# Moving normalizations to ScalarE and sums to GpSimd in a software-pipelined chain of five attentions

## What is computed

```
x1 = LN(x + attention(x, x, causal))            16 heads of 16, rows that are all zero masked
x2 = LN(x1 + attention(x1, ctx))                16 heads of 16
x3 = LN(x2 + (relu(x2 W1 + b1) W2 + b2) * mask)
F, C = LN(x3), LN(ctx)                          the second layer, one head of 256
cross = gelu(softmax(F C') C w1 + c1) w2 + c2
N = LN(cross);  x4 = F + gamma2 * (cross + gamma1 * softmax(N N') N)
x5 = x4 + softmax(x4 ctx') ctx                  the third layer
x6 = x5 + (attention(LN(x5), LN(ctx)) Wo + bo)  8 heads of 32, with biases on q, k, v
u = (LN(x6) Win + bin) B;  s_t = silu(s_{t-1} A') + u_t;  out_t = x6_t + s_t C + mod
```

## Time and profile before

| | before |
|---|---|
| median of 3 runs | 4716.2 us (4705.2 to 4717.8) |
| the profiled execution | 4694.8 us, its span 4693.0 us |
| mean granted TensorE clock | 0.964 |
| busy: PE, DVE, ACT, POOL | 93%, 81%, 59%, 46% |
| before the first group's work / the scan | to about 95 us / from about 4440 us |

### The profile page before, as it was taken

How to read it: one execution, slowest core, us unless ns; L and a number is a source line. 1 busy time by engine, 2 the same in 40 slices (tenths; PEclk the granted TensorE clock), 3 DMA queues, 4 the chain that set the end, 5 groups by cost and what they waited for, 6 DMA issues and landing times. The chain is left out here.

```text
span 4693.0 us, 129503 instructions
## 1 busy us (share of the span) xinstructions
PE 4387.4 (93%) x38563; PEld 3708.0 (79%) x38563; DVE 3780.6 (81%) x10021; ACT 2753.0 (59%) x5761; POOL 2151.9 (46%) x2308
## 2 busy tenths in 40 slices
PE   2899999999999999999999999999999999999758
PEld 1678888888888888888888888888888888887647
DVE  2688888888888888888888888888888888888523
ACT  0466665666666666665666666666666666566411
POOL 0245444444444444444444554444444444454325
PEclk9899999999999999999999999999999999999879
DMA  3000000000000000000000000000000000000045
GB/s 93 17 22 27 29 17 28 26 29 22 24 26 29 29 17 26 29 19 26 26 29 17 29 26 29 17 28 26 29 28 18 29 26 27 18 26 23 16 133 199
DMA packets 139568, 156.21 MB, mean 33 GB/s; under 512 B 23941, under 2 KB 126666, under 8 KB 134858
## 3 DMA queue, kind: packets, MB, share of 16 engines
q1 hardware_dynamic: 139210, 152.93, 10.7%
HBM read 115.01 MB, written 37.88 MB: 33 GB/s over the span
## 5 line engine op out<-in xcount | busy, mean ns | idle before, releaser
L875 ACT ACTIVATE prob<-prob 128x512 f32<-128x512 f32 x1280 | 782.1, 635 | 663.7 <-DVE prob L1030 662.6
L1019 DVE TENSOR_REDUCE mx<-bank 128x4 f32<-128x512 f32 x1280 | 844.5, 682 | 82.0 <-PE bank L598 73.4
L1283 POOL TENSOR_TENSOR rs_ln<-ve_ln,half 128x2 f32<-128x2 f32 x320 | 225.8, 706 | 1436.2 <-DVE ve_ln L998 1436.1
L1030 DVE TENSOR_TENSOR prob<-bank,mx 128x512 f32<-128x512 f32 x1280 | 851.7, 683 | 26.0 <-PE bank L628 7.6
L865 ACT ACTIVATE turned<-bank 128x512 f32<-128x512 f32 x960 | 546.6, 597 | 521.5 <-PE bank L550 400.5
L885 ACT ACTIVATE probT<-bank 128x512 f32<-128x512 f32 x1280 | 722.8, 601 | 179.7 <-PE bank L628 165.0
L628 PE MATMUL bank<-ident,prob 128*128 128x128 f32 x5120 | 780.4, 293 | 13.0 <-ACT prob L875 9.2
L628 PEld LDWEIGHTS bank<-ident,prob 128*128 128x128 f32 x5120 | 627.9, 151 | 104.9 <-issue 46.2
L1330 POOL TENSOR_SCALAR scan_u<-turned,half_of 128x512 f32<-128x512 f32 x256 | 399.4, 1570 | 134.7 <-ACT turned L865 134.7
L1292 POOL TENSOR_TENSOR X<-X,row_ln_g 128x512 f32<-128x512 f32 x192 | 245.5, 1279 | 316.1 <-DVE X L1007 316.1
L598 PE MATMUL bank<-scan_u,turned 32*128 32x256 f32 x4096 | 380.2, 406 | 5.4 <-POOL scan_u L1330 4.9
(11 more groups left out here) (210 smaller groups left out, 8664.7 us busy)
## 6 DMA issues: line engine op xcount, KB each, us to landing
X<-in_x SPq DMA_DIRECT2D x64, 256.0 KB, 3.6
XR<-in_x SPq DMA_DIRECT2D x64, 256.0 KB, 3.8
CB<-in_ctx SPq DMA_DIRECT2D x64, 256.0 KB, 3.6
CC<-in_ctx SPq DMA_DIRECT2D x64, 256.0 KB, 2.6
mod<-mod_rows SPq DMA_DIRECT2D x64, 256.0 KB, 3.4
residual<-X SPq DMA_DIRECT2D x64, 256.0 KB, 3.5
turned<-residual SPq DMA_DIRECT2D x16, 1024.0 KB, 6.8
out<-turned SPq DMA_DIRECT2D x16, 1024.0 KB, 4.8
```

The costliest lines, as they stand in the source:

```text
L875: nc.scalar.activation(flat(t), flat(t), ACT.Exp, scale=SCALE[p]).then_inc(*st["act"].mark(f"exp.{b}{r}"))
L1019: nc.vector.tensor_reduce(m[:], banks.of(f"{att}.tile.{b}{r}")[:, :].rearrange("p (h t) -> p h t", h=4), AX, ALU.max)\
L1030: nc.vector.tensor_tensor(t[:], banks.of(f"{att}.tile.{b}{r}")[:, :].rearrange("p (h t) -> p h t", h=4), maxes.of(f"{att}.max.{b}{r}")[:]. ...
```

## The change

- **Normalizations.** The two `tensor_scalar` on DVE become two ACTIVATEs on ACT, `Identity(rs * x + nmr)`, with `nmr = -mean * rs`. `ve` gets a second instruction, `nmean = -mean` (DVE, 128x2), and POOL a step `nmr` behind `pow` (128x2). Everyone who waited for DVE's normalization waits for ACT's.
- **Residual sums** of the first two attentions move from DVE to POOL, unchanged.
- **The feed-forward bias.** `fc2_bk = fc2_b * mask` (`biased`) and `X2 += fc2_bk` (`x2b`) on POOL; DVE's `bias` pass goes, and `sum` reads the product's bank directly.
- **The values' bias** goes through the output projection once, in the setup: `o_b += v3_b Wo`, with two transposes, a copy and two products. `mix_in.v` becomes an eviction by one ACTIVATE on ACT.
- **The output bias.** `X5 += o_b` on POOL (`x5b`, behind `ln5`), DVE's `obias` pass goes, and `res` reads the bank and adds `X5`.
- **`vp`** is one multiply over both sequences instead of two.
- **New lists** for all engines and new banks. They hold 112 steps on PE (the same), 85 on ACT, 107 on DVE, 41 on POOL. `self_in.len@2` is now the fifth step of PE's list, with bank 4, whose user before it is `self_in.e0`.

The core of the diff; of the lists the parts around the ends of the loops, and of the banks nothing but the two named:

```diff
 PROGRAM = {
     "pe": """
-        ctx_att.back.1@4 ctx_att.back.0@4 self_att.causal.11@2 mix_att.values.02@6 mix_att.values.01@6
...
-        pair.av1@4 mix_att.scores.00@5 ctx_att.turn.11@3 ctx_att.turn.12@3 ctx_att.turn.10@3 pair.yT@4 mix_out.u@6
-        self_in.e0@1 pair.cross@4 ctx_att.values.13@3 ctx_att.values.10@3 ctx_att.values.12@3 ctx_att.values.11@3
-        self_in.len@1 mix_att.turn.01@5 mix_att.turn.00@5 ctx_in.x1T@2 mix_att.turn.02@5 mix_att.turn.03@5
+        ctx_att.values.11@4 ctx_att.values.13@4 ctx_att.values.10@4 ctx_att.values.12@4 self_in.len@2
+        self_att.causal.00@2 ctx_att.back.0@4 mix_att.turn.03@6 mix_att.turn.02@6 ctx_att.back.1@4 ctx_in.x1T@3
+        mix_att.turn.01@6 self_att.causal.01@2 mix_att.turn.00@6 self_att.scores.00@2 self_att.scores.01@2
+        mix_att.values.02@6 mix_att.values.01@6 mix_att.values.00@6 mix_att.values.03@6 pair.ncT@5 ctx_in.q@3
+        pair.sc2@5 ...
+        pair.av1@4 mix_att.scores.00@5 ctx_att.turn.12@3 mix_out.u@6 ctx_att.turn.11@3 ctx_att.turn.10@3
+        ctx_att.turn.13@3 pair.yT@4 self_in.e0@1 pair.cross@4
     "act": """
+        ctx_att.outT.0@4 pair.gelu@5 ctx_att.probT.12@4 self_att.ln1@3 ctx_att.probT.11@4 ctx_att.probT.10@4
+        pair.yT@5 ctx_att.probT.13@4 mix_att.exp.03@6 pair.cross@5 mix_att.exp.02@6 ctx_att.outT.1@4
+        mix_att.exp.01@6 mix_att.probT.03@6 mix_att.exp.00@6 pair.lnN@5 mix_att.probT.02@6 mix_att.probT.01@6
     "dve": """
-        self_in.nz@2 mix_att.centre.00@6 mix_att.max.03@6 mix_att.centre.03@6 pair.lnNstats@5 pair.lnNaggr@5
+        self_in.nz@2 mix_att.centre.00@6 pair.lnNstats@5 pair.lnNaggr@5 pair.lnNve@5 ctx_in.amax@3 ctx_att.recip.0@4
...
+        self_att.ln1aggr@2 pair.a4r@4 pair.a4@4 self_att.ln1ve@2 self_in.keep@1 mix_att.max.03@5 mix_att.max.02@5
+        mix_out.u@6 mix_att.centre.03@5 mix_att.max.01@5 mix_att.centre.02@5 mix_att.centre.01@5 mix_att.max.00@5
     "pool": """
+        self_in.keys@2 self_att.ln1gain@3 self_att.ln1@3 pair.lnNpow@5 pair.lnNnmr@5 pair.lnNgain@5 pair.lnN@5
+        ctx_att.add@4 ctx_in.mask@3 ffn.biased@4 ctx_att.ln2pow@4 ctx_att.ln2nmr@4 ctx_att.ln2gain@4 ctx_att.ln2@4
...
 BANKS = dict(e.split(":") for e in """
-    self_in.len:6 ...
+    self_in.e0:4 self_in.len:4 ...

+                dve.wait_ge(turned_b, 1)
+                nc.vector.tensor_copy(v3_turned[:, 0, :], pbank[6][:, 0:D]).then_inc(turned_b, 1)
+                dve.wait_ge(turned_b, 3)
+                nc.vector.tensor_tensor(rows["o_b"][:], rows["o_b"][:], pbank[7][:, 0:D], ALU.add)

             @block.scalar
+                def norm(key, unit, src, dst, frees):
+                    st = steps[unit]
+                    def go(g):
+                        for w in latest(*(who.before(what, g) for who, what in frees), st["pool"].done(key + "nmr", g)):
+                            act.wait_ge(*w)
+                        for b in range(G):
+                            last = nc.scalar.activation(dst[:, b, :], src[:, b, :], ACT.Identity, bias=nmr[key][:, b:b + 1],
+                                                        scale=rs[key][:, b:b + 1])
+                        last.then_inc(*st["act"].mark(key))
+                    return {key: go}

             @block.vector
+                        nc.vector.tensor_scalar(nmean[key][:], mv[key][:, :, 0], -1.0, None, ALU.mult)
                         nc.vector.tensor_scalar(ve[key][:], mv[key][:, :, 1], EPS, None, ALU.add)\
-                    def apply(g):
...
-                        for b in range(G):
-                            last = nc.vector.tensor_scalar(dst[:, b, :], src[:, b, :], mv[key][:, b, 0:1], rs[key][:, b:b + 1],
-                                                           ALU.subtract, ALU.mult)

             @block.gpsimd
+                    def shift(g):
+                        for w in latest(st["pool"].done(key + "pow", g)):
+                            pool.wait_ge(*w)
+                        nc.gpsimd.tensor_tensor(nmr[key][:], nmean[key][:], rs[key][:], ALU.mult).then_inc(*st["pool"].mark(key + "nmr"))
+                def x2b(g):
+                    for w in latest(ffn["pe"].done("x2T", g), ctx_att["pool"].done("ln2", g), ffn["pool"].done("biased", g)):
+                        pool.wait_ge(*w)
+                    nc.gpsimd.tensor_tensor(nat["X2"][:], nat["X2"][:], fc2_bk[:], ALU.add).then_inc(*ffn["pool"].mark("x2b"))
```

More of the change, by code:

```diff
@@ L139 @@
[L139 to L148, removed]
@@ new lines @@
+        ctx_att.scores.03@3 ctx_att.scores.01@3 ctx_att.scores.02@3 self_att.turn.10@2 self_in.q@1 self_att.back.0@2
+        ctx_in.len@3 self_att.turn.13@2 ctx_in.v@3 self_in.v@1 self_att.values.10@2 self_att.values.13@2
+        self_att.values.11@2 self_att.values.12@2 ctx_att.scores.11@3 ctx_att.scores.12@3 ctx_att.scores.13@3
+        ctx_att.scores.10@3 ctx_att.turn.00@3 ctx_att.turn.01@3 pair.CT@4 self_in.k@1 real.ccT@4 pair.FT@4
+        real.h5T@5 ctx_att.turn.03@3 ctx_att.turn.02@3 self_att.back.1@2 pair.sc1@4 mix_in.q@5 pair.vx@4
@@ L153 @@
+        mix_out.h6T@6 pair.pT1@4 ctx_att.values.00@3 ctx_att.values.02@3 ctx_att.values.01@3 ctx_att.values.03@3
+        pair.av1@4 mix_att.scores.00@5 ctx_att.turn.12@3 mix_out.u@6 ctx_att.turn.11@3 ctx_att.turn.10@3
+        ctx_att.turn.13@3 pair.yT@4 self_in.e0@1 pair.cross@4
     """,
     "act": """
-        ctx_att.probT.12@4 ctx_att.probT.10@4 pair.yT@5 mix_att.exp.01@6 pair.cross@5 mix_att.exp.00@6
-        mix_att.exp.02@6 ctx_att.outT.1@4 mix_att.exp.03@6 mix_att.probT.00@6 ctx_in.x1T@3 mix_att.probT.02@6
@@ L157 @@
[L157 to L161, removed]
@@ new lines @@
+        pair.yT@5 ctx_att.probT.13@4 mix_att.exp.03@6 pair.cross@5 mix_att.exp.02@6 ctx_att.outT.1@4
+        mix_att.exp.01@6 mix_att.probT.03@6 mix_att.exp.00@6 pair.lnN@5 mix_att.probT.02@6 mix_att.probT.01@6
+        mix_att.probT.00@6 ctx_in.x1T@3 mix_out.outT.0@6 self_att.exp.01@2 pair.ncT@5 mix_out.outT.1@6 ctx_in.q@3
+        ctx_in.cT@3 pair.exp2@5 self_att.exp.00@2 ctx_att.ln2@4 pair.pT2@5 ctx_in.k@3 self_att.exp.03@2 ffn.x2T@4
+        self_att.probT.00@2 mix_in.v@5 self_att.probT.01@2 self_in.xT@1 self_att.exp.10@2 real.x4T@5 mix_out.attT@6
@@ L167 @@
+        ctx_att.exp.13@3 real.h5T@5 ctx_att.probT.02@3 ctx_att.probT.03@3 mix_out.ln6@6 self_in.k@1 pair.exp1@4
+        ctx_att.exp.11@3 mix_in.q@5 pair.vx@4 pair.pT1@4 mix_out.h6T@6 ctx_att.exp.10@3
     """,
     "dve": """
-        self_in.nz@2 mix_att.centre.00@6 mix_att.max.03@6 mix_att.centre.03@6 pair.lnNstats@5 pair.lnNaggr@5
-        pair.lnNve@5 self_in.valid@2 pair.lnN@5 ctx_att.recip.0@4 ctx_att.recip.1@4 ctx_att.norm.0@4
-        ctx_att.norm.1@4 ctx_in.amax@3 ctx_att.add@4 ctx_in.keep@3 ctx_att.ln2stats@4 self_att.max.00@2
@@ new lines @@
+    ctx_att.turn.10:1 ctx_att.turn.11:0 ctx_att.turn.12:1 ctx_att.turn.13:7 ctx_att.back.1:6 ffn.x2T:7 ffn.fc1:4
+    ffn.fc2:4 pair.CT:2 pair.FT:3 pair.vx:1 pair.sc1:7 pair.pT1:0 pair.av1:1 pair.yT:2 pair.cross:2 pair.ncT:4
+    pair.sc2:4 pair.pT2:4 pair.av:7 real.x4T:0 real.ccT:5 real.screal:2 real.pTreal:2 real.av:5 real.h5T:4
+    mix_in.k:6 mix_in.v:2 mix_in.q:4 mix_att.tile.00:5 mix_att.tile.01:3 mix_att.tile.02:6 mix_att.tile.03:4
+    mix_att.turn.00:4 mix_att.turn.01:0 mix_att.turn.02:2 mix_att.turn.03:3 mix_out.back.0:7 mix_out.back.1:2
@@ L369, in build @@
         prog_b = nat["NF"]
+        v3_turned = nat["X5"]
         with nc.Block() as block:
@@ L898, in x1r @@
                 def x1r(g):
-                    for w in latest(ctx_att["dve"].before("add", g), self_att["pool"].done("ln1", g)):
+                    for w in latest(ctx_att["pool"].before("add", g), self_att["pool"].done("ln1", g)):
                         act.wait_ge(*w)
```

268 lines of the change are left out of this document (133 added, 135 removed).

## The result

Before: 4710.7 us (median of 4, 4685.0 to 4717.8). The changed kernel: **4760.2 us** (median of 4, 4752.8 to 4765.4), ratio 1.011, interval 1.007 to 1.016: slower by 50 us. The forecast was 4705 in a range from 4580 to 4800, so the time lies inside the range and the sign is wrong.

A forecast was written before the change was run, and what follows sets the result against it. TensorE was taken as the bound. Per round, -0.2 (its work), -0.4 (loop-end wait), +0.7 (new chain), -0.4 (clock) gave -0.3; times 63, -19, plus 8 for ends: 4716 - 11, rounded to 4705 us, range 4580 to 4800.

The forecast's parts named there:

- The bound, and the place of the wait: TensorE bounds the loop; its one wait, 1.49 us per round at the lengths product, comes from DVE's loop turn.
- the allowance for the clock: Loop rounds: 0.4 us per round taken off for less time at the lowered clock.
- The wait at the loop's end: TensorE's lengths product waits for `nz_self` behind DVE's loop turn: 1.4 instead of 1.5 us, in all -0.4 per round.
- the lengths product, which no longer waits for the subtraction: At the loop's end: its new bank, 4, is that of `e0`, so it needs only `nz_self` and starts at +7.3.
- The new chain: `lnN` over DVE, POOL and ACT to TensorE's `ncT`: ready at +14.3, a new wait of 0.7 us, from 0 to 1.2.
- of its 1.0 us I take off 0.4: Lowered clock's cost per round, 1.0 us, reduced by 0.4 because the wait is a little shorter and split over two places.
- Gap gone: Faster rival: DVE's loop-end gap no longer reaches TensorE, -2.2 us per round, 4585 us; chance 0.20.
- the chain's 0.7: Within the faster rival: the `lnN` chain, starting when `cross` is evicted, still costs up to 0.7 us per round.
- ACT late: Slower rival: ScalarE behind the loop's end evicts `cross` 1.5 us late, delaying `lnN` and `ncT`: 4800 us; chance 0.27.
- The held port: DVE's 128x2 `keep` ahead of `max.03`, locked out by GpSimd, delays its stretch up to 0.65 us: about 4740 us.
- Ends: Setup and last, uncovered rounds: extra turns, a product and longer chains, +8 us in all, 0 to 20.

The follow-up runs named there:

- e14: Kernel before with 60 one-column memsets ahead of VectorE's loop, the control to 122 memsets: 4628.0 us.
- e10: Changed kernel, orders untouched, with 20 one-column memsets ahead of VectorE's loop, the control to 75 memsets: 4764.6 us.
- e15: Changed kernel with VectorE's first 35 steps moved to its list's end, plus 48 long-passed waits on TensorE ahead of self_in.len: 4770.0 us, ratio 1.011.
- e11: Kernel before, its own orders, with 122 one-column memsets ahead of VectorE's loop: 4526.8 us, ratio 0.960.
- e13: Changed kernel with VectorE's first 35 steps moved, the eight normalizations back on VectorE, and 44 memsets shifting its loop's start: 4766.8 us.
- e16: Changed kernel with VectorE's first 35 steps moved, plus 48 long-passed waits on TensorE ahead of ffn.fc1: 4735.4 us, ratio 1.005.
- e3: Kernel before with the first 9 steps of VectorE's list moved to its end: 4647.9 us, ratio 0.988.
- e7: Changed kernel with VectorE's first 35 steps moved, plus 24 long-passed waits on TensorE ahead of self_in.len: 4572.3 us (one run).
- e4: Changed kernel with only TensorE's list reordered, self_in.len and the first back product placed later: 4647.5 us, ratio 0.987.
- e2: Changed kernel with the first 35 steps of VectorE's list moved to its end, its loop turn ahead of ffn.relu: 4525.6 us, ratio 0.962.
- e9: Changed kernel, orders untouched, with 75 one-column memsets ahead of VectorE's loop: 4525.1 us, ratio 0.959.
- e12: Changed kernel with VectorE's first 35 steps moved, plus 64 memsets ahead of its loop: 4523.2 us.

## Why the prediction was wrong

- **The bound, and the place of the wait**: right. A full-clock round was forecast at 66.0 + 0.1 (without the allowance for the clock) and is 66.0. TensorE's own work fell from 64.5 to 64.1 (forecast -0.2 from -0.4 to +0.2).
- **The wait at the loop's end**: forecast 1.4 for `nz_self` alone, measured 1.63, and 0.31 more at L690. At full clock the wait for `nz_self` is 1.4, as forecast. The step "the lengths product, which no longer waits for the subtraction" was right; that the first `back` product behind it would was missed (the banks list gives both bank 5). The turn itself grew from 3.3 to 3.6 us.
- **The new chain**: forecast a wait of 0.7 at `ncT`, measured next to none (0.3 us in one round of 56). The chain is ready at +14.3 at full clock, as worked out, and TensorE comes 0.2 us later. TensorE is what I had wrong: from the lengths product to `ncT` it takes 7.2 us at full clock (3096.07 to 3103.28) and not 6.3, since the transpose `x1T` (0.43) and the wait at L690 (0.41) were not counted. In a round with a low stretch it takes 8.7 to 9.6 us; there the chain may be as late as +15.2 (3035.4) and TensorE still comes after it, at +17.1.
- **The step that failed** is the clock: "of its 1.0 us I take off 0.4". Instead of falling to 0.6 it rose to 2.0 us per round (67.99 against 66.0). I had read that the low clock follows the stand and then treated it as a small term in proportion to it; and I let it shrink although my own sum had TensorE standing 1.4 + 0.7 = 2.1 us instead of 1.5 (it stands 1.6 + 0.3). e14, the kernel before, e10, the changed kernel and e15 (stands of 1.0, 1.5, 1.8, 1.9 and 2.1 us: low clock in 16, 38, 55, 52 and 55 of 56 rounds) show that between 1 and 2 us half a microsecond or less takes it from a third of the rounds to nearly all. That, and the higher price of such a round, is the whole loss: 1.0 x 56 us.
- **"Gap gone" as a rival** (0.20, 4585) was the right mechanism with a wrong condition. I tied it to a shorter body ("DVE's list falls only from 120 to 107 steps"), where the start of the body decides. Its time was too high by 60. Its 2.2 us per round do not follow from its terms (1.5 + 1.0 + 0.2 - 0.7 = 2.0), and the gain in the old orders (e11) is 2.9: the chain's 0.7 did not arise, and without the stand a round is 64.0, not 64.5, so TensorE's busy time in a full-clock round with a stand is half a microsecond above what the work needs.
- **ACT late**: the time came nearer to its 4800 than to mine, by luck, since the mechanism did not occur. ScalarE evicts `cross` from +5.8 to +6.4, 0.9 us behind TensorE, and no wait follows; the terms of the forecast add up to +8.45, not to its +7.8, and ScalarE was earlier than both. Its new instructions take 0.59 us each and not 0.42.
- **The held port**: the 128x2 `keep` takes 0.20 us in its new place, not up to 1.1, so the 4740 worked out beside it had no part in this. e13 shows a pair lengthened in this way, 1.51 for 0.73, while GpSimd worked on a pair of 128x512 (3029.95 to 3033.11); that GpSimd is what held it was not tested.
- **Ends**: forecast +8, measured 1.4.

## What to carry to other kernels

Where an engine is late once per round with no releaser but "issue", count the instruction packets on the page before anything else: if they grow with the number of rounds, shift the loop's start by some tens of instructions, and only then judge a change. Here 75 instructions that do nothing made the changed kernel 5% faster and 122 the kernel before 4%, while the redistribution over three engines, judged without them, was worth nothing. In this kernel, which TensorE bounds, a stand of 1 to 2 us per round cost about twice its length (1.7 to 2.3 times, in e14, e10, e15, e16 and the two kernels), since the clock goes with it.

## What was not expected of the hardware

- A loop turn of VectorE is 0.3 us or 2.8 to 3.7 us (3.7 in e3), and for the same body 0.3 or 2.8 to 3.6, by where the body starts; 5 packets of 8 KB per round go with the slow one. No other engine's loop showed it.
- The clock answers to a stand steeply but not by its length alone: 0.8 us idle (e7) lowered it in 18 of 56 rounds, 1.4 us (e4, with waits of 0.9 and 0.2) in none, and e11 with no stand in 4. What else decides stays open.
- TensorE's busy time per round at full clock is not a floor: 64.5 (before), 64.1 (changed) and 64.7 (e4) with a stand, and 63.9 to 64.1 in the variants without one (e2, e9, e11, e12).
